# Attention scores from three bf16 parts, every score and mask matmul divided over four column tiles of 32

## The reference

```python
x = x + 0.5 * ffn(layernorm(x)); x = x + attn(layernorm(x)); x = x + 0.5 * ffn(layernorm(x))

# attn, b=4, l=1024, d=256, 16 heads of 16
qkv = x @ W_qkv.T + b_qkv
scores = einsum('bqhe,bkhe->bhqk', q, k) / 4
scores = where(causal, scores, -inf)
out = einsum('bhqk,bkhe->bqhe', softmax(scores), v)
out = out.reshape(b, l, d) @ W_out.T + b_out
```

## Time and profile before

| | |
|---|---|
| median of 3 runs | 1536.66 us (1536.26 to 1538.86) |
| the profiled execution | 1542.46 us, its span 1540.8 us |
| busy, share of span | PE 86%, PEld 65%, DVE 66%, ACT 50%, POOL 32% |
| softmax stage | about 502 to 1090 us of the span |
| one group in the steady part of it | 33.7 us |
| mean granted TensorE clock | 0.901 of full speed |

### The profile page before, as it was taken

The page is one execution under the profiler, slowest core; times in us unless marked ns, Lnnn a source line. Parts: engine busy times, 40 slices in busy tenths (PEclk is TensorE's granted clock), DMA queues, the critical chain, the costliest instruction groups (busy, mean ns, idle before and its releaser), DMA issues. The chain is left out here.

```text
span 1540.8 us, 31184 instructions
## 1 busy us (share of the span) xinstructions
PE 1325.7 (86%) x8678; PEld 1003.7 (65%) x8709; DVE 1019.6 (66%) x2335; ACT 775.6 (50%) x1949; POOL 496.9 (32%) x651
## 2 busy tenths in 40 slices
PE   2628999899699499999998999999778269998998
PEld 1417999799588255555555555554465159997998
DVE  6594555499866777767675777773286755554787
ACT  2524556333244046666675666666546236564333
POOL 1554444255300201222211112212324554443454
PEclk9658999899899569999998999999896569999999
DMA  6503434122465712223322222200315114433233
GB/s 188 169 3 97 123 123 122 60 73 74 146 233 231 136 30 43 44 43 66 61 44 44 43 43 43 44 2 1 114 35 167 55 59 124 123 123 93 83 112 106
DMA packets 86509, 135.73 MB, mean 88 GB/s; under 512 B 12992, under 2 KB 66176, under 8 KB 83328
## 3 DMA queue, kind: packets, MB, share of 16 engines
q1 hardware_dynamic: 64896, 90.29, 22.1%
q0 software_dynamic: 13056, 35.67, 8.3%
q10 hardware_dynamic: 8448, 8.39, 1.6%
HBM read 81.35 MB, written 52.43 MB: 87 GB/s over the span
## 5 line engine op out<-in xcount | busy, mean ns | idle before, releaser
L1448 DVE TENSOR_REDUCE s_MX<-s_ps_a 128x1 f32<-128x512 f32 (+4 forms) x624 | 368.9, 643 | 133.8 <-PE s_ps_a L1515 132.2
L1422 ACT ACTIVATE s_PR<-s_ps_b 128x512 f32<-128x512 f32 (+3 forms) x768 | 343.7, 491 | 162.3 <-PE s_ps_b L1537 155.2
L1515 PE MATMUL s_ps_a<-s_KO,s_QO 96*128 96x512 f32 (+3 forms) x768 | 286.1, 422 | 22.7 <-DMA s_QO<-qk_scratch 22.7
L1537 PE MATMUL s_ps_b<-s_QO,s_KO 98*128 98x512 f32 (+3 forms) x768 | 266.6, 368 | 7.2 <-issue 3.9
L1391 POOL TENSOR_SCALAR_AFFINE_SELECT s_PR<-s_PR 128x256 f32<-128x256 f32 x256 | 103.5, 407 | 474.5 <-ACT s_PR L1422 473.6
L1537 PEld LDWEIGHTS s_ps_b<-s_QO,s_KO 98*128 98x128 f32 x768 | 146.3, 194 | 72.6 <-ACT s_PR L1422 54.4
L603 POOL DMA_INDIRECT f_XG<-xn_scratch,f_tok_u x144 | 136.4, 947 | 167.3 <-PE f_ps_x L700 157.4
L1515 PEld LDWEIGHTS s_ps_a<-s_KO,s_QO 96*128 96x128 f32 x768 | 152.1, 211 | 28.7 <-DVE s_MX L1448 20.8
L810 POOL DMA_INDIRECT f_YG<-y_scratch,f_slots_u x128 | 121.0, 945 | 150.2 <-DVE X L885 94.6
L1552 PE MATMUL s_ps_o<-s_PR,s_VG 128*17 128x512 f32 (+3 forms) x1536 | 163.0, 496 | 5.3 <-POOL s_PR L1391 5.3
L656 DVE TENSOR_TENSOR f_xl<-f_ps_x,f_xh 128x256 fp32r<-128x256 f32 x144 | 61.1, 425 | 97.7 <-ACT f_xh L628 92.6
(11 more groups left out here) (206 smaller groups left out, 2966.9 us busy)
## 6 DMA issues: line engine op xcount, KB each, us to landing
y_scratch<-f_YS SPq DMA_DIRECT2D x144, 128.0 KB
s_KO<-qk_scratch SPq DMA_DIRECT2D x48, 256.0 KB, 5.8
s_QO<-qk_scratch SPq DMA_DIRECT2D x96, 128.0 KB, 6.6
xn_scratch<-f_XN ACTq DMA_DIRECT2D x16, 512.0 KB, 3.2
qk_scratch<-p_QKh SPq DMA_DIRECT2D x32, 256.0 KB
qk_scratch<-p_QKl SPq DMA_DIRECT2D x32, 256.0 KB
f_stage<-in_w_up SPq DMA_DIRECT2D x20, 352.0 KB
X<-in_x SPq DMA_DIRECT2D x4, 1024.0 KB, 9.4
```

Of the source, the lines that this page charges most:

```text
L1422: nc.scalar.activation(PR[:, u // 2 % SLOTS, u % 2, 0:W - lo], ps_b[u % RING][:, lo:W], ACT.Exp, scale=SCALE).then_inc(exp_done, 1)
L1448: nc.vector.tensor_reduce(MX[:, h:h + heads, i, s], ps_a[v % RING][:, 0:heads * keys].rearrange("p (h n) -> p h n", h=heads), AX.X, ALU.ma ...
L1515: last = nc.tensor.matmul(ps_a[v % RING][:, at:at + keys], QO[k][0:R, h, i * P:(i + 1) * P], KO[k][0:R, h % 2, s * W:s * W + keys], start= ...
L1537: nc.tensor.matmul(ps_b[u % RING][:, lo:W], KO[k][0:RM, h % 2, i * P:(i + 1) * P], QO[k][0:RM, h, hf * W + lo:(hf + 1) * W], start=True, s ...
```

## The change

In the projection each of q and k is now kept as three bf16 parts: ACT rounds (L1118 of the changed kernel), DVE takes the rest in fp32 (`REST`), ACT rounds that to the second part (`part_2`, L1107), POOL subtracts for the third (L1086), and SP writes the three parts with one DMA.

In the softmax stage the operands `QO` and `KO` are bf16, four heads each, with six products of parts (`PAIRS`) on 6 x 16 = 96 rows, and three rows for the maximum (`RM` = 99). No zero rows are needed, and the memsets of `QO` are gone. Each score and mask matmul of 128 output rows becomes four, one for each strip of 32 (`STRIP`), which go to four column tiles, like the product with V. A units are now pairs of heads on a pair of banks (`hp`, `c`): 21 units of up to 1024 columns in a group, and `ps_a` is two slots of two banks. `ps_t` is gone: the turned maxima and the turned output take turns in the same two slots (`USES`, `slot_use`, the semaphore `slot_read`), so that 24 uses pass through two slots in a group. `turn_output` and `turn_max` stand behind the second B unit of their step instead of the fourth. The third part of the maximum needs POOL (`max_rest`), and `place_max` has three DMAs for two; a group's load has 12 DMAs for 9.

```diff
@@ project_stage
-            for n in range(NW * G):
...
-                sp.wait_ge(qkl_done, n + 1)
-                sp.dma_start(qk_dram[w // 2, g, 1, :, cols], QKl[:, g, :].bitcast(F32)).then_inc(qk_out[g], 16)
+                sp.wait_ge(part3_done, n + 1)
+                sp.dma_start(qk_dram[w // 2, g, :, :, cols].rearrange("t p l -> p t l"),
+                             QK[:, g, :, :]).then_inc(qk_out[g], 16)
@@ pool
+            for n in range(NW * G):
+                pool.wait_ge(part2_done, n + 1)
+                nc.gpsimd.tensor_tensor(QK[:, n % G, 2, :], REST[:, n % 2, :], QK[:, n % G, 1, :],
+                                        ALU.subtract).then_inc(part3_done, 1)
@@ act
+            def part_2(n, g):
+                act.wait_ge(rest_done, n + 1)
+                nc.scalar.activation(QK[:, g, 1, :], REST[:, g % 2, :], ACT.Copy).then_inc(part2_done, 1)
@@ dve
-                    dve.wait_ge(qkh_done, G * w + g + 1)
-                    nc.vector.scalar_tensor_tensor(QKl[:, g, :], ps_qk[g % 2][:, :], BQK[:, g:g + 1],
...
+                    dve.wait_ge(part1_done, G * w + g + 1)
+                    if g >= 2 or since(w, 1):
+                        dve.wait_ge(part3_done, G * w + g - 1)
+                    nc.vector.scalar_tensor_tensor(REST[:, g % 2, :], ps_qk[g % 2][:, :], BQK[:, g:g + 1],
+                                                   QK[:, g, 0, :], ALU.add, ALU.subtract).then_inc(rest_done, 1)
@@ softmax_stage
-    PH = 2 * HD
-    R = 3 * PH
-    RM = R + 2
+    PAIRS = ((0, 0), (0, 1), (1, 0), (1, 1), (0, 2), (2, 0))
+    R = len(PAIRS) * HD
+    RM = R + PARTS
+    STRIP = P // 4
...
-            wide = W // keys
-            starts = range(0, GH, wide)
-            A_UNITS += [(i, s, h, min(wide, GH - h), keys) for h in starts]
+            wide = min(W // keys, 2)
+            A_UNITS += [(i, s, hp, wide, keys) for hp in range(0, 2, wide)]
...
     MAX_T = 1 + max(n for n in range(NB) if (1, NA - 1) in A_BESIDE[n])
+    OUT_T = MAX_T - 1
+    USES = []
+    for n in range(NB):
+        beside = [("a",) + one for one in A_BESIDE[n]]
+        USES += beside[:1]
+        if n == 1:
+            USES.append(("out", -1, 1))
+        if n == OUT_T:
+            USES.append(("out", 0, 0))
+        if n == MAX_T:
+            USES.append(("max", 1, 0))
+        USES += beside[1:]
...
-        ps_a = [ps(f"ps_a{i}", [P, W]) for i in range(RING)]
+        ps_a = [ps(f"ps_a{i}", [P, 2, W]) for i in range(2)]
...
-        ps_t = ps("ps_t", [P, W])
@@ sync
-                for part, (q, kk) in enumerate(((0, 0), (0, 1), (1, 0))):
...
+                for part, (q, kk) in enumerate(PAIRS):
+                    rows = slice(part * HD, (part + 1) * HD)
+                    queries = qk_dram[g // G, g % G, q, 0:GF, :].rearrange("(h e c) l -> e h c l", h=2, c=2)
+                    keys = qk_dram[g // G, g % G, kk, GF:2 * GF, :].rearrange("(h e c) l -> e h c l", h=2, c=2)
+                    for operand, src in ((QO[k], queries), (KO[k], keys)):
+                        sp.dma_start(operand[rows, :, :].rearrange("e (h c) l -> e h c l", h=2),
+                                     src).then_inc(operands[k], 16)
...
+                for r, ready in enumerate((max1_done, max2_done, max3_done)):
+                    sp.wait_ge(ready, g + 1)
+                    sp.dma_start(QO[k][R + r:R + r + 1, :, :], NMS[:, r, :]).then_inc(max_rows[k], 16)
             for g in range(4):
-                sp.wait_ge(zeros[g % 2], g // 2 + 1)
-                sp.wait_ge(ones, g + 1)
                 load(g)
@@ pool
-            for k in (1, 3):
-                nc.gpsimd.memset(QO[k][0:RM, :, :].bitcast(F32), 0.0).then_inc(zeros[1], 1)
+            def max_rest(g):
+                pool.wait_ge(slot_read, max_slot(g)[0] + 1)
+                nc.gpsimd.tensor_copy(NMS[:, 1, :], NMR[:, :]).then_inc(max2_done, 1)
+                pool.wait_ge(max2_done, g + 1)
+                nc.gpsimd.tensor_tensor(NMS[:, 2, :], NMR[:, :], NMS[:, 1, :], ALU.subtract).then_inc(max3_done, 1)
...
+                    if n == MAX_T and g + 1 < NG:
+                        max_rest(g + 1)
@@ tensor
-                    if v >= RING or since(g, 1):
-                        pe.wait_ge(a_read, NA * g + v + 1 - RING)
+                    if not isinstance(g, int) or q >= 2:
+                        pe.wait_ge(slot_read, q - 1)
+                    strips = [slice(j * STRIP, (j + 1) * STRIP) for j in range(4)]
...
+                        for c in range(2):
+                            scores = banks[c][:, 0:heads * keys].rearrange("p (h n) -> p h n", h=heads)
+                            for strip in strips:
+                                nc.tensor.matmul(scores[strip, :, keys - P:keys], identb[:, strip], neg[:, 0:heads, :],
+                                                 start=True, stop=False, skip_group_check=True)
+                    for hp in range(hp0, hp0 + heads):
+                        at = (hp - hp0) * keys
+                        for c in range(2):
+                            h = 2 * hp + c
+                            for strip in strips:
+                                last = nc.tensor.matmul(banks[c][strip, at:at + keys],
+                                                        QO[k][0:R, h, i * P + strip.start:i * P + strip.stop],
...
-                nc.tensor.matmul(ps_b[u % RING][:, lo:W], KO[k][0:RM, h % 2, i * P:(i + 1) * P],
-                                 QO[k][0:RM, h, hf * W + lo:(hf + 1) * W], start=True, stop=True).then_inc(b_done, 1)
+                for j in range(4):
+                    strip = slice(j * STRIP, (j + 1) * STRIP)
+                    last = nc.tensor.matmul(ps_b[u % RING][strip, lo:W],
+                                            KO[k][0:RM, h, i * P + strip.start:i * P + strip.stop],
+                                            QO[k][0:RM, h, hf * W + lo:(hf + 1) * W], start=True, stop=True)
+                last.then_inc(b_done, 1)
```

More of the change, by code:

```diff
@@ L23 @@
 TOP_K = 2
+PARTS = 3
 ROUTED_SCALE = 2.5
@@ L1258, in softmax_stage, with slot_use, slot_of_a @@
     MAX_T = 1 + max(n for n in range(NB) if (1, NA - 1) in A_BESIDE[n])
+    OUT_T = MAX_T - 1
[10 more added lines that the diff above has]
+        USES += beside[1:]
+    NU = len(USES)
+    FIRST = NA + 1 + AHEAD
+    def slot_use(g, what, ahead, index=0):
+        at = USES.index((what, ahead, index))
+        if not isinstance(g, int):
+            return FIRST - 1 + NU * g + at, (FIRST - 1 + at) % 2
+        q = FIRST + sum(0 <= n + use[1] < NG for n in range(g + 1) for use in USES[:at if n == g else NU])
+        return q, q % 2
+    def slot_of_a(g, v):
+        if isinstance(g, int) and g * NA + v < NA + AHEAD:
+            q = v + g * (NA + 1)
+            return q, q % 2
+        ahead = 1 if v >= AHEAD else 2
+        return slot_use(g - ahead, "a", ahead, v)
     SLOTS = 6
-    LOAD = 9 * 16
-    PLACE = 2 * 16
-    assert GH == 4 and D // G == 64 and GH * NB % RING == 0 and NB * 2 % SLOTS == 0 and MAX_T < NB
+    LOAD = 2 * len(PAIRS) * 16
+    PLACE = PARTS * 16
+    assert GH == 4 and D // G == 64 and GH * NB % RING == 0 and NB * 2 % SLOTS == 0 and MAX_T < NB and NU % 2 == 0
+    assert all(len(A_BESIDE[n]) <= GH for n in (1, OUT_T, MAX_T))
     with ExitStack() as c:
@@ L1315, in softmax_stage, with max_slot, out_slot @@
         recip = sem("recip")
-        att_done = sem("att_done")
         block = c.enter_context(nc.Block())
+        def max_slot(g):
+            return (NA, NA % 2) if isinstance(g, int) and g == 0 else slot_use(g - 1, "max", 1)
+        def out_slot(g, hf):
+            return slot_use(g + hf, "out", -hf, hf)
         def turn(g, k, back):
@@ L1380, in _ @@
                 prepare(g)
+            max_rest(0)
             for g in range(NG):
@@ L1474, in normalise, with a_beside @@
                     turned[:, :, :, 0:HD], RC[:, :, :].unsqueeze(3).to_broadcast([P, 4, GH, HD]),
-                    ALU.mult).then_inc(att_done, 1)
+                    ALU.mult).then_inc(slot_read, 1)
+            def a_beside(g, groups, v):
+                if until(g, groups, NG):
+                    a_units(g + groups, [v])
+                    if v == NA - 1:
+                        combine(g + 1)
             a_units(0, range(NA))
@@ L1493, in _ @@
                         max_low(g + 1)
+                    for groups, v in A_BESIDE[n][1:]:
+                        a_beside(g, groups, v)
             normalise(NG - 1, 3, 1)
@@ L1500, in a_units @@
                 for v in units:
-                    i, s, h0, heads, keys = A_UNITS[v]
+                    i, s, hp0, heads, keys = A_UNITS[v]
                     diagonal = s == i // 4
+                    q, slot = slot_of_a(g, v)
+                    banks = [ps_a[slot][:, c, :] for c in range(2)]
                     if v == 0:
                         pe.wait_ge(operands[k], LOAD * (quarter(g, k) + 1))
-                    if v >= RING or since(g, 1):
```

(6 more changed lines are left out.)

158 lines of the change are left out of this document (64 added, 94 removed).

## The result

| | before | after |
|---|---|---|
| median, us | 1536.46 (4 runs) | 1566.46 (1563.59 to 1567.71, 4 runs) |
| ratio, 95% interval | | 1.019 (1.0172 to 1.0207) |
| the profiled execution, its span | 1542.46, 1540.8 | 1563.59, 1561.6 |

What follows compares the result with a forecast made beforehand. PE was taken to bound the softmax stage; 6.4 us removed and 4.0 added a group, net -2.4, gave -36 over 15 groups, with -5.5 at the start -41.5: 1495 us from the median, own range 1465 to 1530.

Steps and rivals of the forecast that it cites:

- SP issues 12 loads for 9 ... I cost this at nothing.: Softmax stage, SP: 12 loads for 9 and 3 small DMAs for 2 fit in a group's 31 us; cost nothing.
- Rival 3 (ii), instructions: Softmax stage, PE: at 30 instructions a us a group would take 39.5 us, +120 us; chance 0.05.
- (a): PE, softmax group: drains between full array and column tiles go, 0.20 for each of 12 products; saves 2.4 us.
- (b): PE, softmax group: weight loads that a short matmul cannot cover become hidden; saves 1.8 us.
- (c): PE, softmax group: score matmuls run nearer their bare stream in bf16 than in fp32r; saves 1.2 us.
- (d): PE, softmax group: the present waits for reads go, to be counted anew with the two slots; saves 1.0 us.
- (e): PE, softmax group: transposes alone in the full array between tiled matmuls add drains in three places; costs 0.6 us.
- (g): POOL, step 8 of a group: max_rest comes before the selects, for which the product waits; costs 0.4 us.
- the rule on weight loads: PE, softmax stage: each set of four matmuls waits for its loads, adding 8 us a group, 1615 us; chance 0.04.
- (f): PE, softmax group: waits for DVE to free the two slots, six places of 0.5 us; costs 3.0 us.
- Start of the stage: First loads earlier by 5.8 us, projection's end later by 2.0, first group's A units shorter by 1.7; together -5.5 us.
- Rival 2: PE, softmax group: slot waits twice as long, 6.5 us for 3.0, so 34.8 us a group, 1548 us; chance 0.12.

Runs made afterwards that it cites:

- the line that undoes it: The changed kernel with each load of 16 partitions writing every second partition of a block of 32 instead of 16 neighbours; 1519.87 us, ratio 0.9864.
- The single-bank kernel with strips: The changed kernel with A units in three single banks, a pair of loads a step and every second partition written; 30.68 us a group, ratio 0.9635.
- the best version without the move of the presets: The changed kernel with three single banks, 8 KB pieces, a pair of loads a step, every second partition written, presets still on DVE; ratio 0.9635.

## Why the prediction was wrong

**The step that failed: "SP issues 12 loads for 9 ... I cost this at nothing."** I counted what SP has to issue, and not how the loads run nor who else uses the DMA engines. The three loads of a group that wrote 32 partitions became six of 16 neighbours: the same bytes hold the DMA engines for longer (118 GB/s for 168), and PE's instructions come through the same engines. Priced by the line that undoes it: 1.0190 to 0.9864, 3.3% or 50 us, more than the whole loss. In the profiled executions the 15 groups take 31.5 us less with it, and the first L1588 comes 9.0 us earlier. Of that 4.0 is an earlier begin of the stage, nearly all of it from before the projection and so not the line's doing, and 5 lies in the A units of the first group, where two stalls of 4.2 us together had stood.

**Rival 3 (ii), instructions**, was the right mechanism with the wrong price and, at 0.05, too small a chance. I thought of the rate at which PE can take instructions: 16 in 0.13 us showed it to be high. The limit is the rate at which they arrive, and only while loads run; in the stretch behind the last load 598 matmuls and 594 loads of weights went by in 32.7 us, 36 a us, with no stall. What the prediction lacked was the fetch itself, as a user of the DMA engines. The count of fetches, 59, stood on the page of the kernel before, beside the share of queue q1.

**(a) to (e) and (g), -5.4 forecast, -3.0 measured** (1.8 by the parts, 1.2 by the strips). The single-bank kernel with strips, 30.68 us a group for 33.68, has these terms and no slots: its transposes too stand alone between tiles, and POOL has the third part of the maximum. The kinds were right: B to the next set is 0.215, B to the product likewise, and loads are hidden; the rule on weight loads of the Trainium skill (TensorE: Matmul & The Clock Gate, part 3) would have cost 8 us a group, and the trace disagrees with it once more. Of the 2.4 that are missing, some 0.6 is (g), which I had at 0.4:

```profile
PE s_ps_o L1576 <- POOL s_PR L1408: 21.1, 31, 1.1
```

That is the best version without the move of the presets, 1.3 us a group. Before it was 4.9 us in all, 0.3 a group. Of the two waits a group, the long one, 0.9 to 1.0 us, stands where POOL does `max_rest` before its selects; no run puts `max_rest` behind them. The other 1.8 us stay open: I summed (a) to (d) interval by interval, and argue, without a run for it, that part of each lay beside a wait for ACT or POOL that remains.

**(f), +3.0 forecast, +2.0 measured.** The six places are there: behind the first L1588 there are 91 waits for DVE before A units and turnings, 42 us in 15 groups, 2.8 us and six waits a group. PE in turn waits less for POOL than with single banks, 6.5 us in 16 groups (the row in the result) for 21.1, 0.9 a group, and what is left of the 2.8 is about the 2.0. So the net of a group is -1.0 and not -2.4, 21 us over 15 groups: the second error, and what keeps even the corrected version (1519.87) over the forecast.

**Start of the stage, -5.5 forecast, +7.4 measured.** Three pieces add up to it. The first load goes out at 506.57, 2.6 us earlier than before, for 3.8 forecast: PE ends the projection 1.4 us later, and the last write is issued 3.6 us behind PE's end, for 1.5 before, which was forecast (+2.0). From the first load to the first A unit it takes 15.5 us, for 12.0, at 118 to 120 GB/s; I had this at nothing. From the first A unit to the first L1588 it takes 31.6 us, for 25.1 before and 23.4 forecast. There I took the presets as gone, but three rows of 4096 bf16 take 3.47 us, twice as long as the two rows of 2048 fp32 before (1.76 each), and DVE works on them until 524.6; and two stalls stand in the A units, which take 29.0 us from first read to turning, for 23.7 before.

**Rival 2** came nearest with 1548, and for the wrong reason: its slot waits were to be 6.5 us a group and are 2.8, and the slots alone never made it slower.

## What to carry to other kernels

Before a change multiplies an engine's instructions, divide the count of instruction fetches into the stretch and look at what else the DMA engines do then: a burst of loads that was free can starve it. When a load's destination rows change, look at the packet time and GB/s of its queue, not at its size; neighbouring partitions are the slow choice. And price a change in the steady state apart from what it does to transfers: here the change of the matmuls, 1.9% slower as it stood, became 3.6% faster once one line on the loads, three banks and a wait a step let it through.

## What the runs showed of the hardware

- Instructions arrive 16 KB at a time, one fetch for some 250 matmuls and weight loads of TensorE behind the last load (7 fetches for 1730). With bursts of loads at 118 GB/s a fetch could take 1.9 us and come 12 us behind the last; with bursts at 200 GB/s or a pair of loads at a time gaps stayed under 10.3 us and PE hardly ran dry at 36 instructions a us.
- That the late fetch itself is what PE waits for rests on ten stalls that all ended 1.2 to 1.9 us after a slow fetch had landed, and on five ways of taking the stalls away (fewer instructions, no loads, spread loads, trickling loads, fast loads). No row names it, and that the fetch is late because it stands behind the loads is inferred.
- The same packet of 4096 B took 588 ns into 16 neighbouring partitions and 159 ns into every second of 32 (medians).
- After the stall at 937 us the four column tiles run out of step, in sets of two, for over 4 us, until the next transposes; after those at 897 and 967 us they are in step again at once.
- The time of a memset of 3 rows by 4096 bf16 is 3.47 us on DVE and 3.51 on POOL; 2 rows by 2048 fp32 took 1.76 on DVE. That is some 0.85 ns an element of a row.
